# One VectorE transpose per adjacency tile in a two-layer graph network with a routed feed-forward block

## The reference

```python
def _L0_gnn_ref(x, adj, W1, b1, W3, b3, Wf, bf):
    h = relu(adj @ (x @ W1) + b1)
    h = relu(adj @ (h @ W3) + b3)
    return tanh(h @ Wf + bf)

def _L0_ffn_ref(x, gate_w, W1, W2, W3):
    w, idx = top_k(xt @ gate_w, 2)
    w = softmax(w, axis=1)
    comb = zeros((T, E)).at[arange(T)[:, None], idx].add(w)
    for e in range(8):
        h = silu(xt @ W1[e]) * (xt @ W3[e])
        out = out + h @ W2[e] * comb[:, e:e + 1]

x = x + _L0_gnn_ref(_layernorm(x), adj, ...)
x = x + _L0_ffn_ref(_layernorm(x)[None], ...)[0]
```

## Time and profile before

| what | value |
|---|---|
| median of 3 executions | 612.55 us (612.47 to 614.5) |
| span of the profiled execution | 613.0 us |
| the profiled execution's own time | only the span is given |
| PE busy | 571.9 us, 93% |
| DVE busy | 371.7 us, 61% |
| ACT busy | 295.6 us, 48% |
| granted TensorE clock, mean | 0.995 |
| matrix transposes on VectorE (L1031) | 64, 44.0 us busy |

### The profile page before, as it was taken

The page is one execution under the profiler, slowest core; times in us unless marked ns, Lnnn a source line. Parts: engine busy times, 40 slices in busy tenths (PEclk is TensorE's granted clock), DMA queues, the critical chain, the costliest instruction groups (busy, mean ns, idle before and its releaser), DMA issues.

```text
span 613.0 us, 10885 instructions
## 1 busy us (share of the span) xinstructions
PE 571.9 (93%) x3168; PEld 484.9 (79%) x3169; DVE 371.7 (61%) x796; ACT 295.6 (48%) x553; POOL 145.3 (24%) x143
## 2 busy tenths in 40 slices
PE   0887999999999999999999999999999999999993
PEld 0555888788887878778878898988989889898873
DVE  5998888784657796578653333355333735466571
ACT  2654454665646575576423333354323535365451
POOL 3000000000000506036663413223123231232222
PEclk9999999999999999999999999999999999999997
DMA  9999992000221872430147212126111623646622
GB/s 197 242 203 213 213 211 38 1 1 0 104 69 35 201 236 67 126 112 10 8 101 236 33 31 38 17 40 220 31 26 26 205 59 89 169 96 172 219 34 28
DMA packets 66418, 63.71 MB, mean 104 GB/s; under 512 B 5915, under 2 KB 60829, under 8 KB 66365
## 3 DMA queue, kind: packets, MB, share of 16 engines
q1 hardware_dynamic: 57724, 52.32, 34.5%
q0 software_dynamic: 8224, 10.53, 10.4%
q10 hardware_dynamic: 432, 0.39, 0.2%
HBM read 54.02 MB, written 10.26 MB: 105 GB/s over the span
## 4 chain that ended last, share of the span: by engine, by line
PE 79%; SPq 6%; DVE 5%; issue 4%; DMA 3%; ACT 2%; POOL 1%; POOLq 0%; ACTq 0%; DVEq 0%
PE bank L1618 27%; PE bank L1644 14%; PE bank L1494 8%; PE bank L1495 8%; PE bank L1496 8%; SPq L388 4%; PE bank L1672 4%; PE bank L1523 2%; PE bank L1507 2%; PE bank L1469 2%; SPq L379 1%; DMA adj_s<-in_adj 1%; PE bank L1611 1%; PE bank L1520 1%; PE bank L1547 1%
## 5 line engine op out<-in xcount | busy, mean ns | idle before, releaser
L1618 PE MATMUL bank<-ew,xeT 128*128 128x512 f32 x840 | 202.2, 395 | 1.9 <-DVE ew L1340 1.4
L1618 PEld LDWEIGHTS bank<-ew,xeT 128*128 128x128 f32 x840 | 154.6, 188 | 33.5 <-issue 2.4
L1494 PE MATMUL bank<-ring,Z 128*128 128x512 f32 x256 | 104.3, 408 | 23.3 <-DVE ring L993 23.0
L1644 PE MATMUL bank<-ew,heT 128*128 128x256 f32 x840 | 109.2, 286 | 3.6 <-issue 2.4
L1644 PEld LDWEIGHTS bank<-ew,heT 128*128 128x128 f32 x840 | 102.9, 191 | 5.3 <-issue 3.7
L993 DVE TENSOR_TENSOR ring<-adj_s,ring 128x512 fp32r<-128x512 f32 x128 | 85.7, 679 | 29.6 <-ACT ring L642 28.6
L1496 PE MATMUL bank<-ring,Z 128*128 128x512 f32 x256 | 101.0, 394 | 0.0
L1495 PE MATMUL bank<-ring,Z 128*128 128x512 f32 x256 | 100.9, 394 | 0.0
L642 ACT CAST ring<-adj_s 128x512 fp32r<-128x512 f32 x128 | 77.0, 623 | 36.9 <-PE bank L1496 23.9
L523 POOL DMA_INDIRECT slot_rows<-val,route x32 | 35.7, 1116 | 203.6 <-issue 199.7
L556 POOL DMA_INDIRECT out<-y_st,idx_st x29 | 45.4, 1565 | 161.4 <-ACT y_st L807 158.1
(11 more groups left out here) (187 smaller groups left out, 534.0 us busy)
## 6 DMA issues: line engine op xcount, KB each, us to landing
w_raw<-in_L_ffn_W SPq DMA_DIRECT2D x24, 1024.0 KB, 5.5
adj_s<-in_adj SPq DMA_DIRECT2D x64, 256.0 KB, 6.1
x_in<-in_x SPq DMA_DIRECT2D x16, 128.0 KB, 6.0
x_res<-in_x SPq DMA_DIRECT2D x4, 512.0 KB, 3.5
out<-x SPq DMA_DIRECT2D x4, 512.0 KB, 4.1
ffn_in_rows<-x_res SPq DMA_DIRECT2D x4, 512.0 KB, 3.1
xg<-ffn_in_rows,idx POOLq DMA_INDIRECT x39, 3.0
Wg<-in_L_gnn_W SPq DMA_DIRECT2D x2, 256.0 KB, 8.4
```

Of the source, the lines that this page charges most:

```text
L1494: nc.tensor.matmul(a, zh, hi, start=(jb == 0), stop=False)
L1618: last = nc.tensor.matmul(out_ap, stat[:, sl, k, :], w_at(k, wl), start=(k == k0 and sl == wl == 0), stop=(k == k1 - 1 and sl == 1))
L1644: last = nc.tensor.matmul(y_p[:, 0:D], heT[:, sl, k, :], ew[:, o + 2 * H * wl + D * k:][:, 0:D], start=(k == sl == wl == 0), stop=(k == KH ...
```

## The change

`turn(p)` returns at once for the first three quarters of a tile. At the fourth it turns all 2048 columns in one instruction and adds 4 to `s_turn`.

```diff
 
             def turn(p):
 
+                if p % CT < CT - 1:
+                    return
                 n = p // CT
                 dve.wait_ge(s_adj[n % NC], QUADS * (n // NC + 1))
-                v = adj_s[:, n, CW * (p % CT):CW * (p % CT + 1)]
-                nc.vector.transpose(v, v).then_inc(s_turn, 1)
+                v = adj_s[:, n, :]
+                nc.vector.transpose(v, v).then_inc(s_turn, CT)
```

## The result

The changed kernel takes **617.63 us** (median of 4, 617.29 to 618.28), the one before 612.51 us (median of 4, 611.86 to 614.5). The ratio is 1.008, with a 95% interval of 1.0063 to 1.0098: slower by 5.1 us, where +1.8 us had been forecast and the range ended at 616.8.

The account below looks back on a forecast made before the run. TensorE was taken to bound the kernel (79% of the 613.0 us span), with VectorE leading up to 55.33 us. The terms -1.8 + 3.6 gave +1.8 us on 612.55, so 614.3 us, range 610.6 to 616.8.

Parts of the forecast that it names:

- The size of the instruction: On VectorE, one 128x2048 transpose lasts 2.32 us and holds the next instruction off 2.24 us, against 2.48 for four.
- the rival in which all of it is saved: Each wide transpose saves the whole fixed part of three quarters: hold 2.01 us, kernel 612.3 us; chance 0.12.
- Part one: Up to W1_rows of chunk 0 at 55.33 us, where VectorE leads TensorE: a gain of 1.8 us.
- Tile 5: here the first quarter waited for the DMA ... 1.68 us: At tile 5 on VectorE, other work now goes ahead and covers a DMA wait of 1.68 us.
- the 0.22 us at tile 4: At tile 4 on VectorE, the later wide transpose avoids a gap, probably for the tile's landing: -0.22 us.
- T: Time a wide transpose holds off VectorE's next instruction: 2.24 us, counted nine times over in the sum.
- Part one, tiles 0 to 4: VectorE up to lo(15): -0.17 for tile 0, +0.72 for tiles 1 to 3, -0.46 for tile 4, sum +0.09 us.
- The waits of x_lo: In tiles 1 to 3, x_lo waits uncovered for ScalarE's x_hi, 0.44 us each; +0.72 us in all for these tiles.
- the faster rival: Neither the later TensorE stalls nor the waits at x_lo come: 609.4 us; chance 0.06.
- Part two: TensorE stalls at W1_rows of chunks 1 and 2 and at product 59: 1.18 + 1.18 + 1.25, a loss of 3.6 us.
- The rival that the stalls do not come: VectorE's own waits or TensorE's queue take up the three later stalls: 610.7 us; chance 0.10.
- the slower rival: The wide transpose costs what four cost apart, holding VectorE 2.49 to 2.80 us: 616.6 to 619.4 us; chance 0.15.

Follow-up runs that it names:

- four_narrow: The changed kernel with four 128x512 transposes issued together in place of each wide one: 618.64 us, ratio 1.0088.
- before_again: The kernel before, unchanged, run again for a second trace: 612.96 us, ratio 1.0003.
- after_again: The changed kernel, unchanged, run again for a second trace: 616.43 us, ratio 1.0066.
- keep_warm: The changed kernel with six unused matmuls on TensorE ahead of W1_rows of chunk 0: 616.24 us, ratio 1.0048.
- wide_early: The kernel before with only tiles 0 to 4 turned by a wide transpose, in the changed kernel's places: 613.26 us, ratio 1.0011.
- behind_adj: The changed kernel with the wide transposes of tiles 5, 9 and 13 moved behind adj_x_lo: 611.67 us, ratio 0.9985.
- placed: The changed kernel with all 16 transposes wide, at places chosen from the traces: 609.67 us, ratio 0.994.
- after_load: The changed kernel with an extra 512 KB DRAM-to-DRAM DMA ahead of tile 5's loads: 618.13 us, ratio 1.0085.
- after: The changed kernel as first measured against the one before: 617.63 us, ratio 1.008.
- after_swap: The changed kernel with tile 6's loads issued ahead of tile 5's: 619.07 us, ratio 1.0089.
- quarters_three: The changed kernel with tiles 9, 13 and 15 turned in quarters as before: 614.51 us, ratio 1.0031.
- before_load: The kernel before with an extra 512 KB DRAM-to-DRAM DMA ahead of tile 5's loads: 613.01 us, ratio 1.0008.
- before_swap: The kernel before with tile 6's loads issued ahead of tile 5's: 617.20 us, ratio 1.006.

## Why the prediction was wrong

**The size of the instruction: right.** 2.304 us against 2.32, and the next instruction 2.23 us after its start (44.70 to 46.93) against 2.24. The starts decided, not the durations: of the fixed part only 0.25 us a tile was saved (2.48 less 2.23), and about 0.2 against four in a row, as four_narrow shows. So the rival in which all of it is saved gave too much here. The Trainium skill, "VectorE: DVE Perf Modes", "The TRN2 errata — SBUF-src ops pay a fixed extra latency per instruction", says that many small tiles pay the fixed part each; the estimate of 0.47 us a tile that the prediction drew from it was too much as well.

**Part one, the step that failed: "Tile 5: here the first quarter waited for the DMA ... 1.68 us".** The wait was in the trace and would have been covered, as the pair with the swapped loads shows (0.94 us against 4.10). But I took it, and the 0.22 us at tile 4, for a property of the kernel, and before_again has neither. So the gain of 1.8 us that part one had in the sum isn't there. Without the two the step reads -1.83 + 1.68 + 0.22 = +0.07 us; measured, between before_again and after_again, +0.21. With that in place of -1.8 the whole sum reads +3.7 us, 616.2, which after_again (616.43) and keep_warm (616.24) took. The prediction saw that the span lay 0.45 us above the median, and went on to form its difference in that trace. It did not ask whether the traced execution was like the others, though a span is the shorter of the two. That after_again lies inside the stated range is luck: the range reached so far up for a T of 2.49 us, and T was 2.23.

**What is left of the first comparison.** It came out 1.2 us above after_again. In the one execution of it that was traced (617.29 us) tile 0 landed 1.0 us later than in after_again. Two of the others (617.97 and 618.28) had the lower mean clock, of which more below. The fourth (617.30) left no trace, so its cause stays open.

**Part one, tiles 0 to 4: right.** +0.09 had been reckoned up to lo(15), with the 0.22 us at tile 4; without these +0.3, and it was +0.38 between the traces of wide_early and before_again, +0.5 in the medians. The waits of x_lo cost what had been reckoned, so the faster rival is out.

**Part two: right.** 1.18, 1.18 and 1.25 us were forecast, 0.97, 1.12 and 1.28 measured; behind_adj removes the first two by place alone; the third goes in placed, with two tiles moved at once. The rival that the stalls do not come is out. So is the mechanism of the slower rival: the kernel is slower by more than 0.5%, but not through T.

**What no step had: the clock.** The change stretches TensorE's gap ahead of W1_rows from 1.4 to 2.2 us, and in 4 of 10 executions the mean clock is lower and the time about 1.7 us longer. The first comparison had two such among its four. The trace of after_load shows such a drop at this place. That drop cost 1.6 us, as much as lies between the two groups. That the other executions lost their time at the same place was not seen, since they left no trace; keep_warm makes it likely, no more.

## What to carry to other kernels

Before a forecast is built on one trace, hold its span against the times of the other executions: a DMA wait in a single trace may be the luck of that execution, and a change that "covers" it has no gain to show in the median. Joining small instructions into a wide one saves a little at each joint and, at the worst place, holds up whatever stands behind it for its whole length; look at what stands directly behind it in the engine's order and for whom that is due, and move the wide one past it. Here the same 16 instructions cost 3.7 us at one set of places and gain 3.1 us at another.

## What the runs showed of the hardware

TensorE's granted clock fell from 2.4 to 1.2 GHz after gaps of 2.04 us (after, at 41.45 us), 2.19 (after_load, at W1_rows) and 3.21 (after_swap). It did not fall after every gap of that length: 2.15 in after_again, 2.19 in after and in quarters_three and 2.33 in four_narrow, all at the same W1_rows, left it at full speed. Where TensorE is the bound, such a drop cost 1.6 us (after_load) and 2.8 us (after_swap). With six matmuls put into the gap, none of six executions was of the longer kind.

On VectorE an in-place transpose of 128x512 float32 lasts 0.698 us and one of 128x2048 2.304 us, 1.05 ns a column; the next instruction starts 0.62 and 2.23 us after their start, before their recorded end. A 512 KB copy from DRAM to DRAM ahead of the loads did not make VectorE wait for tile 5 (before_load), while swapping the loads of tiles 5 and 6 made it wait 4.1 us (before_swap).
